# A vision tower's second mixture of experts: GpSimd adds the LayerNorm's rows to the residual, ScalarE copies one of the two output banks

## The reference

```python
h = gelu(patches(x) @ weight + bias)
h = h + relu_attention(layernorm(h))
h = h + mixture_0(layernorm(h))      # 6 experts, three matrices each, top 2
h = h + rope_attention(layernorm(h)) # one head, causal softmax
h = h + mixture_1(layernorm(h))      # 8 experts, two matrices each, top 2
```

```python
out = tokens
for e in range(8):
    y = gelu(tokens @ w1[e] + b1[e]) @ w2[e] + b2[e]
    out = out + combine[:, e:e + 1] * y
```

## Time and profile before

| | |
|---|---|
| median of three runs | 636.5 us (632.03, 636.5, 637.41) |
| the profiled execution | 640.04 us, its span 638.2 us |
| TensorE busy | 587.9 us (92%), 6943 matmuls |
| VectorE busy | 497.5 us (78%) |
| ScalarE busy | 308.6 us (48%) |
| GpSimd busy | 148.9 us (23%) |
| mean granted TensorE clock | 0.966 |

### The profile page before, as it was taken

The page is one execution under the profiler, slowest core; times in us unless marked ns, Lnnn a source line. Parts: engine busy times, 40 slices in busy tenths (PEclk is TensorE's granted clock), DMA queues, the critical chain, the costliest instruction groups (busy, mean ns, idle before and its releaser), DMA issues.

```text
span 638.2 us, 17652 instructions
## 1 busy us (share of the span) xinstructions
PE 587.9 (92%) x6943; PEld 372.5 (58%) x6943; DVE 497.5 (78%) x1503; ACT 308.6 (48%) x738; POOL 148.9 (23%) x151
## 2 busy tenths in 40 slices
PE   0999999999998899999999888999998999999993
PEld 0995565558986644444444346777777454555441
DVE  2747788967795967799887765888888899988863
ACT  0010000014442356776776746787876555566651
POOL 1000000765564121051100323314422221321000
PEclk9999999999996979999999999999997799999998
DMA  8998768210000000000000000000000000000111
GB/s 279 412 388 313 275 225 270 52 21 2 3 1 2 1 2 3 1 2 3 2 1 3 2 1 2 2 2 2 1 2 1 2 22 22 21 21 23 23 24 29
DMA packets 28899, 39.21 MB, mean 61 GB/s; under 512 B 19984, under 2 KB 20368, under 8 KB 28816
## 3 DMA queue, kind: packets, MB, share of 16 engines
q1 hardware_dynamic: 27016, 36.87, 16.8%
q10 hardware_dynamic: 1800, 1.20, 0.8%
HBM read 35.37 MB, written 2.69 MB: 60 GB/s over the span
## 4 chain that ended last, share of the span: by engine, by line
PE 75%; DVE 14%; issue 4%; ACT 4%; DMA 2%; SPq 0%; DVEq 0%; ACTq 0%
PE bank L415 18%; PE bank L1594 9%; PE bank L1632 5%; PE bank L1634 4%; PE bank L1025 3%; PE bank L1606 3%; PE bank L1657 3%; PE bank L1075 3%; DVE m_hm L1894 3%; PE bank L1039 2%; PE bank L812 2%; PE bank L1617 2%; PE bank L1583 2%; DMA image<-in_x_dram 2%; PE bank L1033 2%
## 5 line engine op out<-in xcount | busy, mean ns | idle before, releaser
L579 POOL TENSOR_TENSOR centred<-h,mean 82x512 f32<-82x512 f32 x64 | 71.1, 1111 | 422.3 <-DVE rstd L562 229.0
L415 PE MATMUL bank<-cols,tok_weight 64*64 64x328 f32 (+1 forms) x1800 | 116.0, 414 | 16.2 <-DVE cols L459 15.1
L1463 ACT ACTIVATE m_h<-bank,m_b 128x656 f32<-128x656 f32 x112 | 90.4, 807 | 80.8 <-PE bank L1594 80.4
L1894 DVE TENSOR_TENSOR m_hm<-bank,m_h 128x656 f32<-128x656 f32 x112 | 94.0, 839 | 29.4 <-PE bank L1606 26.1
L415 PEld LDWEIGHTS bank<-cols,tok_weight 64*64 64x64 f32 x1800 | 77.0, 137 | 50.7 <-issue 17.2
L1594 PE MATMUL bank<-m_xt,m_w 64*64 64x328 f32 x896 | 90.4, 474 | 0.0
L458 DVE COPY cols<-image 128x1992 f32<-128x1992 f32 x32 | 62.1, 1950 | 17.5 <-DMA image<-in_x_dram 14.7
L1632 PE MATMUL bank<-m_hm,m_wo 64*64 64x328 f32 x512 | 48.4, 447 | 3.0 <-DVE m_osb L1901 2.3
L392 ACT ACTIVATE tok_fm<-bank,tok_bias 128x328 f32<-128x328 f32 x16 | 7.7, 531 | 86.1 <-PE bank L415 86.1
L984 ACT ACTIVATE sa_prob<-sa_masked,sa_low 82x82 f32<-82x82 f32 x128 | 44.6, 350 | 8.0 <-DVE sa_low L1129 8.0
L1470 ACT ACTIVATE m_h<-bank,m_b 128x328 f32<-128x328 f32 x96 | 45.7, 528 | 3.6 <-PE bank L1617 3.6
(11 more groups left out here) (184 smaller groups left out, 1044.1 us busy)
## 6 DMA issues: line engine op xcount, KB each, us to landing
image<-in_x_dram SPq DMA_DIRECT2D x32, 1000.0 KB, 10.7
out_dram<-m_fin SPq DMA_DIRECT2D x16, 164.0 KB
tok_weight<-in_L_tok_weight_dram ACTq DMA_DIRECT2D x2, 400.0 KB, 8.6
m_w<-in_L_ffn_w_dram SPq DMA_DIRECT2D x2, 128.0 KB
m_sel_raw<-c_sel_dram SPq DMA_DIRECT2D x1, 256.0 KB
m_w<-in_L_ffn_expert_w_dram SPq DMA_DIRECT2D x2, 96.0 KB
m_wo<-in_L_ffn_expert_w_dram SPq DMA_DIRECT2D x4, 48.0 KB
m_sel_raw<-c_sel_dram SPq DMA_DIRECT2D x1, 192.0 KB
```

Of the source, the lines that this page charges most:

```text
L415: return pe.matmul(sum_bank[u % 2][s][t * D:(t + 1) * D, L * j0:L * j1], weight[s * R:(s + 1) * R, c, :], cols[u % 2][s * R:(s + 1) * R, c ...
L579: pool.tensor_tensor(self.centred[:], slots(self.h, g), mean.broadcast_to([L, G, D]), ALU.subtract).then_inc(self.shifted, 1)
L1463: act.activation(h1[n % RING][:], h1_bank, ACT.Gelu if last else ACT.Relu, bias=W.b1[:, k:k + 1]).then_inc(h1_ready, 1)
L1894: dve.tensor_tensor(hm[k][:], cb_bank, src[n % RING][:], ALU.mult).then_inc(hm_ready, 1)
```

## The change

In the second mixture the turned rows `xt` are no longer added to the output. Instead GpSimd adds the rows `xn` of each group to `h` in place (`with_input`), and `residual` then adds `h` as before. For this the mixtures' LayerNorms get six buffers for rows instead of three (`KEPT`), and `residual` waits for the addition (`with_rows`). GpSimd's addition for group g stands ahead of `normalise(g + 6)`; it waits for `normed` of that group, and the pair of them for the first `weigh` of step g, as `normalise(g + 6)` did before. The wait of the second mixture's `normalise(f)` for `x_turned` is now one for the turn of group f - 6, and for f = 3, 4 and 5 there is none. ScalarE copies the odd bank to a tile `odd` (`copy_odd`, after the second GELU of a step and before `copy_x`), and VectorE's output is one addition of the even bank and `odd`.

```diff
--- before.py
+++ after.py
@@ -43,6 +43,8 @@
 NBLOCK = L + (PW - 1) // SW
 MULTIPLY_IN, SCALE_IN = (2, 3), (4, 5)
 RING = 3
+
+KEPT = 6
 AHEAD = 3
 
 
@@ -171,7 +173,8 @@
         moe = [moe_weights(nc, A, sb, sem, layer) for layer in (0, 1)]
 
         shared = (h, stats, mean, rstd, tmp, centred)
-        xn = [[sb(f"xn{i}{p}", [L, G * D]) for p in range(3)] for i in (0, 1)]
+
+        xn = [[sb(f"xn{i}{p}", [L, G * D]) for p in range((3, KEPT)[i])] for i in (0, 1)]
         norm = []
         for i in range(4):
             norm.append(LayerNorm(sem, f"ln{i}", shared, xn[i % 2], i % 2 == 0, norm[-1] if i else None, (6, 10, NG) if i % 2 else (NG // 2, 3 * NG // 4, NG)))
@@ -569,7 +572,7 @@
 
     def rows(self, g):
 
-        return self.xn[g % 3][:].rearrange("p (b d) -> p b d", d=D)
+        return self.xn[g % len(self.xn)][:].rearrange("p (b d) -> p b d", d=D)
 
     def normalise(self, pool, g):
 
@@ -1334,6 +1337,7 @@
     h2 = None if last else [sb(f"h2_{n}", [128, 2, HALF]) for n in range(RING)]
     hm = [sb(f"hm{k}", [128, 2, HALF]) for k in range(NP)]
     osb = sb("osb", [128, HALF])
+    odd = sb("odd", [128, HALF]) if last else None
     unused = sb("unused", [L, 1])
 
     lg = [sb(f"lg{p}", [L, 2 * G, E]) for p in (0, 1)]
@@ -1379,7 +1383,8 @@
     hm_ready = sem("hm_ready")
     o_pairs = sem("o_pairs")
     o_done = sem("o_done")
-    o_even = sem("o_even")
+    with_rows = sem("with_rows")
+    odd_ready = sem("odd_ready")
     o_ready = sem("o_ready")
     o_turned = sem("o_turned")
     added = sem("added")
@@ -1399,14 +1404,27 @@
                 sp.wait_ge(sent[p], NG // 2 * 16)
 
     def gpsimd(pool):
+        def with_input(g):
+
+            pool.wait_ge(normed, g + 1)
+            pool.tensor_tensor(slots(h, g), slots(h, g), mine.rows(g), ALU.add).then_inc(with_rows, 1)
+
         def step(f):
-            wait(pool, x_turned, f - 2)
-            if last and f > FRONT + 1:
+            if not last:
+                wait(pool, x_turned, f - 2)
+            elif f > FRONT + 1:
 
                 pool.wait_ge(hm_ready, NP * (f - FRONT - 2) + 1)
+                with_input(f - KEPT)
+                pool.wait_ge(x_turned, f - KEPT + 1)
+                pool.wait_ge(with_rows, f - KEPT + 1)
             mine.normalise(pool, f)
 
         in_groups(step, AHEAD)
+        if last:
+            for g in range(NG - KEPT, NG):
+                pool.wait_ge(hm_ready, NP * g + 1)
+                with_input(g)
         if following is not None:
             pool.wait_ge(normed, NG)
             for f in range(AHEAD):
@@ -1469,6 +1487,11 @@
             for s in (0, 1):
                 ins = act.activation(h2[n % RING][:, s, :], h2_bank[:, s, :], ACT.Relu, bias=W.b2[:, s, k:k + 1])
             ins.then_inc(h2_ready, 1)
+
+        def copy_odd(g):
+            act.wait_ge(o_done, g + 1)
+            wait(act, o_ready, g)
+            act.activation(odd[:], o_banks[1], ACT.Copy).then_inc(odd_ready, 1)
 
         def output(g):
             act.wait_ge(o_done, g + 1)
@@ -1524,11 +1547,15 @@
                 if k == COMBINE and exists(g + 1):
                     combine(g + 1)
                 if last:
+                    if k == 0 and exists(g - 1):
+                        copy_odd(g - 1)
                     if k == 0 and g and exists(f):
                         copy_x(f)
                     if g % 2 and k < 3 and exists(g + 1):
                         round_part((g + 1) // 2, k)
-        if not last:
+        if last:
+            copy_odd(NG - 1)
+        else:
             yield
             output(NG - 1)
 
@@ -1896,14 +1923,15 @@
         def output(g):
             dve.wait_ge(o_done, g + 1)
             wait(dve, o_turned, g)
-            dve.tensor_tensor(osb[:], o_banks[0], xt[g % len(xt)][:], ALU.add).then_inc(o_even, 1)
-            dve.wait_ge(o_even, g + 1)
-            dve.tensor_tensor(osb[:], o_banks[1], osb[:], ALU.add).then_inc(o_ready, 1)
+            dve.wait_ge(odd_ready, g + 1)
+            dve.tensor_tensor(osb[:], o_banks[0], odd[:], ALU.add).then_inc(o_ready, 1)
 
         def residual(g):
             dve.wait_ge(o_turned, g + 1)
             if last and g >= 2:
                 dve.wait_ge(sent[g % 2], g // 2 * 16)
+            if last:
+                dve.wait_ge(with_rows, g + 1)
             dst = fin[g % 2][:] if last else slots(h, g)
             dve.tensor_tensor(dst, back[0:L, :].rearrange("p (b d) -> p b d", d=D), slots(h, g), ALU.add).then_inc(added, 1)
```

## The result

The changed kernel takes 640.89 us (median of 14 runs, 637.92 to 643.99), the kernel before 635.28 (14 runs beside them, 631.88 to 637.41). The ratio is 1.0085, 95% interval 1.0063 to 1.0108: slower, by 0.85% or some 5.4 us. The profiled execution took 640.93 us, its span is 638.9, the mean granted clock 0.968. Its trace can be laid beside that of before almost as it is, since the profiled execution of before was a long one for that kernel (640.04).

A forecast was written before the change was run, and what follows sets the result against it. Early full-stretch groups: TensorE and VectorE both nearly full; later groups: TensorE's pace; last four steps: waits for osb. -1.1 + 1.0 + 1.6 = +1.5 us on a median of 636.5 gave 638.0 us, range 632.5 to 643.5.

The forecast's parts named there:

- the three terms: Last four steps -1.1, GpSimd additions in the full stretch +1.0, early normalisations in the second attention +1.6: +1.5 us.
- rival (b): TensorE's stop in the second attention, near 468 us, drops its clock to 1.2 GHz: +5 more, 643 us; chance 0.17.
- The last four steps: Steps 12 to 15: the sum in osb comes 0.31 us sooner four times, -1.2, taken as -1.1; other bound 0.
- The sum is ready 0.18 after the start: Step 12: finish_sum's sum ready at 599.06, so the copy runs 599.10 to 599.55 and VectorE's addition from 599.59.
- The additions in the full stretch: Steps 1 to 5: GpSimd's additions block VectorE, three steps lose about 0.4 each; +1.0 us, bounds -1.6 and +1.8.
- Step 5 was to run as before: Second mixture, step 5: the three GpSimd operations run as late as before.
- After step 5 VectorE takes up such a delay: Second mixture after step 5: VectorE waits for TensorE in every step, so GpSimd's delays are absorbed; steps still 8.22 us.
- The saving on VectorE: First five groups lose 1.6 us to a full VectorE; winning all of it back was the bound, -1.6.
- The attention: Second attention: early normalisations hold up VectorE's mask by 2 to 3 us, so TensorE loses +1.6; bounds 0, +2.5.
- The alternation: VectorE and GpSimd take turns, one VectorE operation per GpSimd operation; by the lock alone attention's cost would be 0, not 1.6.
- (a): The lock is harmless, attention's slack takes the normalises and VectorE wins back 1.6: -2.8, 633.7 us; chance 0.17.
- (c): ScalarE's copy delays copy_x in all 11 groups: +3.7 on top, 641.7 us; chance 0.05.

The follow-up runs named there:

- e2: The changed kernel without the 16 GpSimd additions; the copy of the odd bank and early normalisations stay: 638.4 us, ratio 1.0037 to the kernel before.
- e8: The changed kernel with the GpSimd addition's second operand replaced by the broadcast mean, so its output is wrong; one execution, 640.27 us.
- e5: The kernel before with six row buffers and normalisations 3 to 5 paced, one pair of GpSimd operations per group of the second attention: 636.06 us, ratio 1.0000.
- e9: The changed kernel with normalisations 3 to 5 paced, one pair per group of the second attention: 638.81 us, ratio 1.0056 to the kernel before.
- e1: The changed kernel with normalisations 3 to 5 put back behind their wait for x_turned: 639.55 us, ratio 1.0067 to the kernel before.
- e3: The kernel before with only KEPT = 6 and the early normalisations, no GpSimd additions or ScalarE copy: 639.46 us, ratio 1.0060.

## Why the prediction was right in sign and range, and where its sum failed

The forecast was +1.5 us on 636.5, and +5.4 came on 635.3. The range and the sign hold, the size doesn't: it is over three times the forecast. The three runs of before were on the long side by 1.2 us, which hid a part of the error, and the bounds of the three terms alone end at 640.8, just below the 640.89 measured. That the range goes on to 643.5 it owes to rival (b).

**The last four steps, -1.1 forecast, +0.2 measured.** This step of the working failed. "The sum is ready 0.18 after the start" was taken from the chain, where 628.30 is the last piece of L1643; the matmuls of this `finish_sum` start at 628.12 in the order of time. So the banks can be read 0.36 after the start, not 0.18; my copy started at 599.10, 0.22 behind, and the real one at 599.69, 0.36 behind 599.33. Then I let VectorE follow ScalarE after 0.04 (599.55 to 599.59); it is 0.14 (600.13 to 600.27). 0.14 + 0.10 of the 0.31 were never there, and 0.08 is what step 12 shows (1.58 instead of 1.66 from `finish_sum` to `sum_pair`); before's last two waits were 0.55 already, so that there 0.02 is left. e2 has what is left without additions: -0.17 for all four, nearly all of it in the first two. The GpSimd addition in step 13 then costs 0.36 (7.95 us, 7.59 around it). I had seen it and given it 0.1.

**The additions in the full stretch, +1.0 forecast, +1.9 measured** (the term's bound was 1.8). The mechanism is as put down: three GpSimd operations in a row, L1846 at 0.74 in the odd step (+0.45, forecast 0.5), L1860 at 1.02 in the even one (+0.74, forecast 0.4 to 0.8), step 4 unharmed, TensorE waiting for `weigh` in its place. Step 5 was to run as before; it takes 9.26 us where e2 has 8.31, so the additions cost most there. The size was off because I priced L1410 by L579 and L586, whose second operand is a broadcast; e8 shows that at 1.04 us the stretch would have come out at +1.2. "After step 5 VectorE takes up such a delay" was wrong by 0.48 us for the same reason: with 1.04 it is 0.02. Both figures of e8 come from one trace.

**The saving on VectorE.** I had expected nothing of it where GpSimd blocks, and all of it, 1.6, as the bound. Timed at `finish_sum` the whole loss is 2.2 (43.34 - 5 x 8.22); the starts of L1899 gave 1.6 because its start in step 1 is already 1.13 us behind `finish_sum`. e2 measures 0.89 with the blocks gone, and nearly all of it in step 5.

**The attention, +1.6 forecast, +1.3 measured.** Right, place and row included: L1142 waits for the fourth operation, two small ones are caught by the last two, and L1036 waits 1.20 us for L1122. The alternation, one held-up VectorE operation per GpSimd operation, is what the sum needed (L546 shows that a small one can slip through between them); the Trainium skill's page "SBUF — State Buffer" (section "Who interferes with whom") gives the lock, and by the lock alone this term would have been 0.

**Rival (b) had the right cause in the wrong place.** The clock doesn't fall at the stop, as I wrote, but the stop is followed by more half clock at the hand-over, 39.6 us a run instead of 28.7. I had given it 0.17 as a case of its own; it is a part of what happened. e5 and e9 show that taking the stop away takes the extra half clock away, in two kernels; e1 shows it in part. Of the 2.2 us between the changed kernel and e9, 1.3 are the stop; the 0.9 left come with 11 us more half clock, most of it in the hand-over, where VectorE and ScalarE set the pace too. The same subtraction between e3 and e5 leaves 2.7 us for 13 us more half clock, so the price of the clock is known only roughly. The Trainium skill's page "TensorE: Matmul & The Clock Gate" (Part 1) says that low activity halves the clock. In this trace the 10 us with the stop are at 1.00, although TensorE is busy for 8.80 of them only:

```profile
460.00:470.00 10.00, 8.80 (x80) 6.83 (x79) 9.40 (x28) 6.32 (x25) 1.50 (x2) 1.00 0.01 2
```

From 470 to 480 the clock is 1.00 too; it is low from 480 on. In before's trace as well the stretch from 482 to 484, which I put beside the page, is itself at 1.00, and the clock is 0.50 only from 490 to 500.

**(a) and (c) fell.** `copy_x` kept its time, and from step 6 on e2's steps are 8.22.

**The account.** Steps +2.6, stop +1.3, clock about +0.9, 0.2 outside the span (640.84 - 638.83 against 1.81 in the mean): 5.0 of 5.6. The 0.6 left I can't place; e9 has 0.4 of the kind (3.4 against 2.8 + 0.14). The clock term is a remainder of a subtraction and not measured by itself: if the account is to close it would be 1.5, and by the 0.37 us that go with 0.001 of clock within one kernel's runs it would be 3.1 for the 0.0085 between before and changed.

## What to carry to other kernels

Moving work to an idle engine isn't free when its operations and those of the full engine wait for each other: look where the row of its operations ends, put each beside the other engine's PSUM reads or statistics, and keep the row off a group in which the other engine has several operations with both inputs in SBUF. Pacing the row by a semaphore of that group was enough here (e5, e9). Price an operation by a row with the same operands, a broadcast one being another operation, and read a start from the order of time, not from a chain's piece. A hand-over between two engines that saves a half-microsecond operation has to bring its own delay, here 0.36 and 0.14; let both engines read the banks at the same time instead of one after the other.

## What the runs showed of the hardware

- A GpSimd addition of 82x512 f32 takes 1.27 us with two full operands and 1.04 with one broadcast over 64 elements (16 of each).
- GpSimd is held up as well: L582 took 1.31 us beside L1142's 1.49. In the kernel before L1139 started first (456.06) and kept its 0.69 us, and GpSimd's L579 took 1.45.
- A stop of TensorE of 1.2 us near 463 us moved the mean time at half clock from 28.7 to about 40 us a run, and the shortest of all runs from 21.4 to 30.5; the granted clock is 1.00 at the stop and low in the hand-over from 480 us on, where it is low in the kernels without the stop too, for 9.8 us on average in eight traces instead of 19.6 in four. Within the runs of one kernel 0.001 less of mean clock goes with 0.37 us more.
